# Image attention: scores in two banks of 333 columns, with the high queries on the keys' low halves as two products of 64 rows

## The chip, the cores and the metric

The program runs on one core of a Trainium2 chip. The metric is device time in microseconds (us) of one execution; given is the median of several. Matmuls run on TensorE (PE; its weight loads are listed apart as PEld), elementwise work on VectorE (DVE), ScalarE (ACT) and GpSimd (POOL); SyncE (SP) issues most DMA transfers. TensorE writes to PSUM, called `banks` here: eight banks of 512 fp32 columns on 128 partitions.

## The reference

The kernel computes four layers, each a gated attention followed by a gated feed-forward part, on an x of 4 batches by 512 tokens by 128. The change touches the first attention alone:

```python
def _L0_xattn_ref(image_embeds, latents, ln1_g, ln1_b, ln2_g, ln2_b, Wq, Wkv, Wo):
    DIM_HEAD, HEADS = 64, 16
    x = layer_norm(image_embeds, ln1_g, ln1_b)      # 4 x 154 x 128
    l = layer_norm(latents, ln2_g, ln2_b)           # 4 x 512 x 128
    q = l @ Wq
    kv = jnp.concatenate([x, l], axis=1) @ Wkv      # 666 keys
    k, v = jnp.split(kv, 2, axis=-1)
    # to heads: 4 x 16 x tokens x 64
    scale = 1.0 / np.sqrt(np.sqrt(DIM_HEAD))
    w = jnp.einsum('bhqd,bhkd->bhqk', q * scale, k * scale)
    w = jax.nn.softmax(w.astype(jnp.float32), axis=-1).astype(q.dtype)
    out = jnp.einsum('bhqk,bhkd->bhqd', w, v)
    return out.transpose(0, 2, 1, 3).reshape(B, S_lat, INNER) @ Wo

x = x + jnp.tanh(g_xattn[0]) * _L0_xattn_ref(ctx_1024, _layernorm(x, axis=-1), ...)
```

## The kernel before

The first attention ("image attention") is worked off in 32 groups (`GROUPS0`: 4 batches by 8 pairs of heads). A group has eight **subtiles** (256 in all, `SUBS`; number i): head 0 or 1 of the pair, and one of four tiles of 128 queries. Every subtile needs the scores of 128 queries against 666 keys (`KEYS0`: 512 of the tokens and 154 of the image), then a softmax and the product with the values.

fp32 accuracy is had from bf16 matmuls: queries and keys are split into a high half (the value rounded to bf16) and a low half (what is left). A head is 64 deep and the array has 128 rows, so one pass holds two products. For head h, `q[n % 2][:, h, :]` has the queries' high half in 64 of its rows and their low half in the other 64. `k[n % 2][:, h, part, :]` has the keys' high half (part 0) or low half (part 1) in both halves of the rows. A pass over part 0 and one over part 1 add up all four products of halves, in `image_scores_pe` (lines 741 to 750): four matmuls (L749), of 512, 512, 154 and 154 columns, all with the same 128 by 128 stationary operand. The columns 0 to 511 lie in one bank, 512 to 665 in the next; two such slots of two banks take turns.

The order of work is written out by hand; engines wait for one another through semaphores (`wait_ge`, `then_inc`). The loop of `image_pe` over steps i does on TensorE:

- the scores of subtile i (L749);
- in odd steps, for one head of an earlier unit of four subtiles, the product of the probabilities with the values (`image_weigh_pe`: L788, 30 small matmuls, sometimes L794 behind them);
- the turn of the probabilities of subtile i - 2 (`image_turn_pe`): four fp32 transposes into bank 4 (L760), one or more into bank 5 (L767, L769, L772);
- in even steps, one part of the projections for the next group (L520).

Bank 4 has one buffer. ACT copies it out (L947), and the next four transposes wait for that copy (`kept_a`).

DVE takes the negated maximum of the scores (L832), ACT the exponential with it as bias (L954); both read the 666 columns of a slot as one run. POOL splits the turned probabilities into halves (L1055) and gathers the last 32 of every row (L1061). For the next group ACT and DVE cut the projections into halves (L977, L914 for the queries; L983, L918 for the keys), and SP moves them between partitions: three transfers of 64 partitions for q (lines 1102 to 1105), four for k (L1109: two per head, 2664 bytes on each of 64 partitions). The first score of a group and head waits until the transfers of that head have landed (`in_place`).

In the part that follows and in later layers the kernel has matmuls with fewer than 128 rows or columns of the array in use. The profile shows them as rows*columns: 128*128 is the whole array, 128*64 and 128*32 fewer columns, 64*128 the upper 64 rows. L2993, L3024, L3025 and L2977 of the last layer are such lines and their neighbours.

## Time and profile before

| | |
|---|---|
| median of 3 runs | 1662.7 us (1659.42 to 1669.96) |
| the profiled execution | 1668.15 us |
| its span, first to last instruction | 1666.3 us |
| mean granted TensorE clock | 0.946 of full |
| score matmuls | from 34.9 to 636.9 us of the span |

The profile is of one execution; all rows below are of it. Times in its views are us from the start of its span, unless marked ns. The matmuls are pipelined: the next one starts while the last columns of the one before are still on their way through the array, so the distance from start to start tells what a matmul costs in a stream, and its own duration is longer than that. A row of several merged instructions shows the time from the first start to the last end.

### The profile page before, as it was taken

What the parts mean: (1) busy time and instruction counts of PE and PEld (TensorE: products, weight loads), DVE (VectorE), ACT (ScalarE), POOL (GpSimd) and SP (SyncE); (2) the same over time, 40 slices, a digit from 0 to 9 for tenths busy, and PEclk for the clock granted to TensorE, in tenths of its full rate; (3) what the DMA queues carried; (4) which work ended last, traced back from release to release, by engine and by line L of the source; (5) the groups of instructions that cost most, each with busy time, mean ns of one, the idle gap of its engine ahead of it and who ended that gap; (6) DMA issues with size and microseconds to landing.
All of it is one profiled execution on the core that took longest, in us unless ns stands there. A gap on an engine that the chain in (4) does not pass through costs nothing.

```text
span 1666.3 us, 37005 instructions
## 1 busy us (share of the span) xinstructions
PE 1448.2 (87%) x13825; PEld 979.5 (59%) x13825; DVE 1115.8 (67%) x2918; ACT 780.2 (47%) x1565; POOL 878.1 (53%) x1308
## 2 busy tenths in 40 slices
PE   3999999999999998887888789989986777789997
PEld 2777777777777776655566545544453343435555
DVE  4889788878777675544664577755454657587763
ACT  2777767767775562543223445554234444311211
POOL 3789888978776694364225663414014322253330
PEclk9999999999999999998999999999997789988998
DMA  7233222211121121241000000000000000000000
GB/s 276 69 118 93 87 86 53 52 45 47 46 61 44 44 63 44 61 150 42 1 1 1 9 9 2 2 1 1 1 1 1 1 1 1 1 0 1 7 7 14
DMA packets 35479, 64.31 MB, mean 39 GB/s; under 512 B 7535, under 2 KB 25042, under 8 KB 34147
## 3 DMA queue, kind: packets, MB, share of 16 engines
q1 hardware_dynamic: 33831, 59.83, 12.2%
q8 instruction: 113, 1.85, 0.5%
q0 software_dynamic: 1472, 2.12, 0.4%
q14 instruction: 63, 0.52, 0.1%
HBM read 30.64 MB, written 12.66 MB: 26 GB/s over the span
## 4 chain that ended last, share of the span: by engine, by line
PE 33%; DVE 12%; ACT 3%; POOL 3%; issue 2%; DMA 0%; DVEq 0%; ACTq 0%; POOLq 0%
PE banks L520 9%; PE banks L2202 3%; PE banks L2188 2%; PE banks L3050 2%; PE banks L2709 1%; PE banks L2993 1%; PE banks L2155 1%; PE banks L2715 1%; DVE work L2285 1%; PE banks L495 1%; PE banks L1755 1%; PE banks L2191 1%; PE banks L2977 1%; DVE work L3213 1%; DVE xn L466 1%
## 5 line engine op out<-in xcount | busy, mean ns | idle before, releaser
L1055 POOL TENSOR_TENSOR work<-work 128x512 bf16<-128x512 f32 (+1 forms) x512 | 358.7, 723 | 78.2 <-ACT work L947 77.3
L832 DVE TENSOR_REDUCE work<-banks 128x1 f32<-128x666 f32 x256 | 216.4, 845 | 65.1 <-PE banks L749 62.5
L954 ACT ACTIVATE work<-banks,work 128x666 f32<-128x666 f32 x256 | 208.1, 813 | 31.8 <-DVE work L832 24.9
L947 ACT ACTIVATE work<-banks 128x512 f32<-128x512 f32 x256 | 152.8, 597 | 146.5 <-PE banks L760 146.1
L460 POOL TENSOR_TENSOR norm_room<-norm_room,minus_half 128x4 f32<-128x4 f32 (+1 forms) x56 | 53.1, 950 | 289.6 <-DVE norm_room L435 168.8
L749 PE MATMUL banks<-work 128*128 128x512 bf16 (+1 forms) x1024 | 188.8, 307 | 3.8 <-DMA work<-work 3.7
L760 PE MATMUL banks<-const,work 128*128 128x128 f32 x1024 | 159.6, 279 | 15.4 <-ACT work L947 12.2
L520 PE MATMUL banks<-work,weights_b 128*128 128x512 bf16 (+1 forms) x840 | 152.8, 340 | 9.9 <-ACT work L1340 4.3
L749 PEld LDWEIGHTS banks<-work 128*128 128x128 bf16 x1024 | 96.2, 98 | 83.1 <-DMA work<-work 4.7
L2285 DVE TENSOR_REDUCE work<-banks 128x2 f32<-128x308 f32 x192 | 86.4, 471 | 83.0 <-PE banks L2155 58.3
L788 PE MATMUL banks<-work 128*128 128x65 bf16 (+1 forms) x3840 | 136.5, 193 | 3.1 <-POOL work L1055 1.8
L760 PEld LDWEIGHTS banks<-const,work 128*128 128x128 f32 x1024 | 111.6, 142 | 35.3 <-issue 34.3
L788 PEld LDWEIGHTS banks<-work 128*128 128x128 bf16 x3840 | 129.1, 97 | 3.8 <-POOL work L1055 3.4
L520 PEld LDWEIGHTS banks<-work,weights_b 128*128 128x128 bf16 (+1 forms) x840 | 81.5, 98 | 76.4 <-issue 12.5
L3262 POOL TENSOR_TENSOR work<-work 128x512 bf16<-128x512 f32 x64 | 67.5, 1060 | 98.7 <-DVE work L3213 98.6
L2260 ACT ACTIVATE work<-banks 128x256 f32<-128x256 f32 (+1 forms) x256 | 88.5, 380 | 62.3 <-PE banks L2191 34.9
L840 DVE COPY work<-banks 128x128 f32<-128x128 f32 x256 | 73.3, 286 | 28.4 <-PE banks L769 14.9
L2188 PE MATMUL banks<-work 128*128 128x256 bf16 (+1 forms) x256 | 69.7, 292 | 9.2 <-ACT work L2252 5.3
L495 PE MATMUL banks<-const,xn 128*128 128x128 f32 x176 | 32.2, 307 | 48.7 <-DVE xn L466 19.9
L769 PE MATMUL banks<-const,work 128*128 128x128 f32 x256 | 70.2, 274 | 0.5 <-DVE scratch L1203 0.5
L2155 PE MATMUL banks<-work 128*128 128x308 bf16 x192 | 60.0, 317 | 7.6 <-DVE work L2285 7.5
L501 ACT ACTIVATE xt<-banks 128x512 f32<-128x512 f32 x28 | 16.7, 597 | 104.8 <-PE banks L495 104.8
(460 smaller groups left out, 3289.6 us busy)
## 6 DMA issues: line engine op xcount, KB each, us to landing
work<-work SPq DMA_DIRECT2D x128, 166.5 KB, 2.7
sorted<-in_pads SPq DMA_DIRECT2D x10, 838.5 KB
weights_b<-in_weights SPq DMA_DIRECT2D x1, 4120.0 KB, 23.8
work<-scratch SPq DMA_DIRECT2D x64, 64.0 KB, 1.9
weights_b<-in_weights SPq DMA_DIRECT2D x1, 2824.0 KB, 12.3
weights_a<-in_weights SPq DMA_DIRECT2D x1, 2056.0 KB
weights_a<-in_weights SPq DMA_DIRECT2D x1, 2050.0 KB, 9.9
work<-work SPq DMA_DIRECT2D x32, 64.0 KB, 1.9
```

The costliest lines, as they stand in the source:

```text
L520: m = pe.matmul(out, left(a), right(b), start=start and n == 0, stop=stop and n == 2)
L749: m = pe.matmul(slot[:, a:z], lhs, k[:, h, part, a:z], start=part == 0, stop=part == 1)
L760: m = pe.transpose(ps[:, t * P:(t + 1) * P], prob[:, t * P:(t + 1) * P], self.eye)
L788: pe.matmul(self.out_heads[:, 2 * j + h, 0:width], parts[:, h, t, j * P:(j + 1) * P, of_probs], v[:, t, of_values, h, 0:width], start=(h, ...
L832: ve.tensor_reduce(self.neg_max[i % 4], self.slot[i % 2][:, 0:KEYS0], AX_X, ALU.max, negate=True).then_inc(self.mark("max"))
L947: ac.activation(self.probs_t[u % 2][:, h, 0:4, j * P:(j + 1) * P], self.bank_a.rearrange("p (t n) -> p t n", t=4), ACT.Copy).then_inc(self ...
L954: ac.activation(self.probs[i % 3], self.slot[i % 2][:, 0:KEYS0], ACT.Exp, bias=self.neg_max[i % 4]).then_inc(self.mark("exp"))
L1055: po.tensor_tensor(parts[:, :, :, 0], exact, parts[:, :, :, 1], ALU.subtract).then_inc(self.mark(event, i - 3))
L2155: m = pe.matmul(bank, a.q4[b % 2][:, group, c * P:(c + 1) * P], a.keys[b % 3][:, 2 * g:2 * g + 2, :].rearrange("p h k -> p (h k)"), start= ...
L2188: m = pe.matmul(bank, left, a.q4[b % 2][:, g, cols], start=True, stop=s != 4)
L2260: ac.activation(out, self.bank_of(k, HALF)[0:rows_n, :], ACT.Exp).then_inc(self.mark("exp4", s, n))
L2285: ve.tensor_reduce(a.most[u % 2][:, c % 2, 2 * g:2 * g + 2], self.bank_of(a.score_banks[n % 3], 2 * CTX).rearrange("p (h k) -> p h k", h=2 ...
```

## The change

The keys' low halves are no longer held in both halves of the rows. `k[n % 2][:, h, :]` now has 666 columns with the high halves of all keys in both halves of the rows, and 334 columns behind them: in the upper 64 rows the low halves of the keys 0 to 333, in the lower 64 rows those of the keys 332 to 665. The scores of a subtile lie in two banks: keys 0 to 332 at the columns 1 to 333 of the first, keys 333 to 665 at the columns 1 to 333 of the second. They are made by four matmuls of 334 columns. Two use all 128 rows of the array (both halves of the queries on the keys' high halves, one for each bank). Two use 64 rows: the queries' high half on the low halves of the keys, the first in the upper 64 rows for the first bank, the second in the lower 64 rows for the second bank. The product of low half with low half is left out. The built program gives the last two the array positions (0, 0) and (64, 0), each 64 by 128. For a high half on each side of the partitions, the queries' high half is kept whole in a buffer of its own, `q_both`; the queries' low half is written straight into `q`, so that `q_part` and its two waits go. DVE's maximum and ACT's exponential read the two banks as 2 by 333. SP's transfers for k become six: per head one of 1000 columns, one of 666 and one of 334.

```diff
@@ -15,6 +15,7 @@
 I32 = mybir.dt.int32
 U16 = mybir.dt.uint16
 AX_X = mybir.AxisListType.X
+AX_XY = mybir.AxisListType.XY
 
 P = 128
 BATCH, SEQ, CTX = 4, 512, 154
@@ -37,6 +38,7 @@
 PAIRS = H0 // 2
 KEYS0 = SEQ + CTX
 KT0 = -(-KEYS0 // P)
+PART0 = KEYS0 // 2
 EXPERTS, FF = 8, 512
 ROOM = 10
 SORT, SORTED = 256, 15
@@ -564,11 +566,11 @@
     def image_memory(self):
         self.work_at = self.stage0_at
         self.q = [self.place(2, SEQ, dt=BF16) for _ in range(2)]
-        self.k = [self.place(2, 2, KEYS0, dt=BF16) for _ in range(2)]
+        self.q_both = [self.place(SEQ, dt=BF16) for _ in range(2)]
+        self.k = [self.place(2, KEYS0 + PART0 + 1, dt=BF16) for _ in range(2)]
         self.v = [self.place(KT0 + 1, 2, 2 * VALUE, dt=BF16).rearrange("p t s (h d) -> p t s h d", h=2) for _ in range(3)]
         self.probs = [self.place(KEYS0) for _ in range(3)]
         self.k_parts = self.place(2, KEYS0, dt=BF16)
-        self.q_part = self.scratch[:, 2:4, :].rearrange("p t n -> p (t n)").bitcast(BF16)
         self.probs_t = [self.place(2, KT0 - 1, 2 * P) for _ in range(2)]
         self.rest, self.rest_t = ([self.place(P) for _ in range(2)] for _ in range(2))
         self.ctx_last = self.place(2, P + 32, dt=BF16)
@@ -735,7 +737,11 @@
 
     def in_place(self, n, h):
 
-        return self.at(f"dma_head{n % 2}{h}", 48 * (n // 2 + 1))
+        return self.at(f"dma_head{n % 2}{h}", 64 * (n // 2 + 1))
+
+    def scores_of(self, i):
+
+        return self.slot[i % 2].rearrange("p (k n) -> p k n", k=2)[:, :, 1:PART0 + 1]
 
     def image_scores_pe(self, pe, i):
         u, n, b, p, h, j = self.image_sub(i)
@@ -743,10 +749,14 @@
         if i % 8 in (0, 2):
             pe.wait_ge(*self.in_place(n, h))
         slot = self.bank(pe, 2 * (i % 2), "exp", i + 1, n=2)
-        lhs, k = self.q[n % 2][:, h, qt * P:(qt + 1) * P], self.k[n % 2]
-        for a, z in ((0, SEQ), (SEQ, KEYS0)):
-            for part in (0, 1):
-                m = pe.matmul(slot[:, a:z], lhs, k[:, h, part, a:z], start=part == 0, stop=part == 1)
+        rows, k = slice(qt * P, (qt + 1) * P), self.k[n % 2][:, h, :]
+        first, second = slot[:, 1:PART0 + 2], slot[:, BANK:BANK + PART0 + 1]
+        whole, both = self.q[n % 2][:, h, rows], self.q_both[n % 2][:, rows]
+        top, bottom = slice(0, D0), slice(D0, 2 * D0)
+        pe.matmul(first, whole, k[:, 0:PART0 + 1], start=True, stop=False)
+        pe.matmul(second, whole, k[:, KEYS0 - PART0 - 1:KEYS0], start=True, stop=False)
+        pe.matmul(first, (both, whole)[h][top, :], k[top, KEYS0:], start=False, stop=True)
+        m = pe.matmul(second, (whole, both)[h][bottom, :], k[bottom, KEYS0:], start=False, stop=True)
         m.then_inc(self.mark("scores"))
 
     def image_turn_pe(self, pe, i):
@@ -829,7 +839,7 @@
                                  ALU.mult).then_inc(self.mark("divided"))
             if i < SUBS:
                 ve.wait_ge(*self.at("scores", i + 1))
-                ve.tensor_reduce(self.neg_max[i % 4], self.slot[i % 2][:, 0:KEYS0], AX_X, ALU.max, negate=True).then_inc(self.mark("max"))
+                ve.tensor_reduce(self.neg_max[i % 4], self.scores_of(i), AX_XY, ALU.max, negate=True).then_inc(self.mark("max"))
             if i >= 1 and (i - 1) // 8 + 1 < GROUPS0 and (i - 1) % 8 in (0, 2, 4, 6):
                 self.image_lows_ve(ve, (i - 1) // 8 + 1, (i - 1) % 8 // 2)
             if 2 <= i < SUBS + 2:
@@ -908,10 +918,7 @@
             return
         if part == 0:
             ve.wait_ge(*self.at("q_high", n + 1))
-            if n >= 1:
-                for h in (0, 1):
-                    ve.wait_ge(*self.in_place(n - 1, h))
-            ve.scalar_tensor_tensor(self.q_part, side, D0 ** -0.5, self.q[n % 2][:, 0, :], ALU.mult, ALU.subtract).then_inc(self.mark("q_low"))
+            ve.scalar_tensor_tensor(self.q[n % 2][:, 1, :], side, D0 ** -0.5, self.q_both[n % 2], ALU.mult, ALU.subtract).then_inc(self.mark("q_low"))
         else:
             k, c0, width = self.k_parts, (0, SEQ)[part - 1], (SEQ, CTX)[part - 1]
             ve.wait_ge(*(self.at("k_high", 2 * n + 1) if part == 1 else self.at("v_kept", 4 * n + 3)))
@@ -951,7 +958,7 @@
                     ac.wait_ge(*self.at("turned_b", i - 1))
                     ac.wait_ge(*self.at("gathered", i - 3))
                 ac.wait_ge(*self.at("max", i + 1))
-                ac.activation(self.probs[i % 3], self.slot[i % 2][:, 0:KEYS0], ACT.Exp, bias=self.neg_max[i % 4]).then_inc(self.mark("exp"))
+                ac.activation(self.probs[i % 3].rearrange("p (k n) -> p k n", k=2), self.scores_of(i), ACT.Exp, bias=self.neg_max[i % 4]).then_inc(self.mark("exp"))
             if i == 4:
                 ac.wait_ge(*self.at("dma_rows", 16))
                 ac.activation(self.gates[:, :], self.rows[:, 0:8], ACT.Tanh).then_inc(self.mark("gates"))
@@ -974,7 +981,7 @@
         if part == 0:
             if n >= 2:
                 ac.wait_ge(*self.at("scores", 8 * n - 8))
-            ac.activation(self.q[n % 2][:, 0, :], side, ACT.Copy, scale=D0 ** -0.5).then_inc(self.mark("q_high"))
+            ac.activation(self.q_both[n % 2], side, ACT.Copy, scale=D0 ** -0.5).then_inc(self.mark("q_high"))
         elif part in (1, 2):
             c0, width = (0, SEQ)[part - 1], (SEQ, CTX)[part - 1]
             if part == 1 and n >= 1:
@@ -1097,16 +1104,17 @@
         self.loads(sp)
         top, bottom = slice(0, D0), slice(D0, 2 * D0)
         for n in range(GROUPS0):
-            q, k, low = self.q[n % 2], self.k[n % 2], self.q_part
+            q, both, k, parts = self.q[n % 2], self.q_both[n % 2], self.k[n % 2], self.k_parts.rearrange("p s n -> p (s n)")
             sp.wait_ge(*self.at("q_low", n + 1))
-            sp.dma_start(q[top, 1, :], q[bottom, 0, :]).then_inc(self.mark("dma_swap", n=16), 16)
-            sp.dma_start(q[bottom, 1, :], low[bottom, :]).then_inc(self.mark(f"dma_head{n % 2}1", n=16), 16)
+            sp.dma_start(q[top, 0, :], q[top, 1, :]).then_inc(self.mark("dma_swap", n=16), 16)
+            sp.dma_start(q[bottom, 0, :], both[top, :]).then_inc(self.mark(f"dma_head{n % 2}0", n=16), 16)
             sp.wait_ge(*self.at("dma_swap", 16 * (n + 1)))
-            sp.dma_start(q[bottom, 0, :], low[top, :]).then_inc(self.mark(f"dma_head{n % 2}0", n=16), 16)
+            sp.dma_start(q[top, 1, :], both[bottom, :]).then_inc(self.mark(f"dma_head{n % 2}1", n=16), 16)
             sp.wait_ge(*self.at("k_low", 2 * n + 2))
             for h, own in ((0, top), (1, bottom)):
-                for half in (top, bottom):
-                    sp.dma_start(k[half, h, :, :], self.k_parts[own, :, :]).then_inc(self.mark(f"dma_head{n % 2}{h}", n=16), 16)
+                sp.dma_start(k[top, h, :], parts[own, 0:KEYS0 + PART0 + 1]).then_inc(self.mark(f"dma_head{n % 2}{h}", n=16), 16)
+                sp.dma_start(k[bottom, h, 0:KEYS0], parts[own, 0:KEYS0]).then_inc(self.mark(f"dma_head{n % 2}{h}", n=16), 16)
+                sp.dma_start(k[bottom, h, KEYS0:], parts[own, 2 * KEYS0 - PART0 - 1:]).then_inc(self.mark(f"dma_head{n % 2}{h}", n=16), 16)
             if 2 <= n < 2 + PAD_PARTS:
                 self.pads_sp(sp, n - 2)
 
```

On PE, two subtiles in a row in the middle of a group, the second with the product with the values behind it. Before (L749 scores, L760 and L769 turn, L520 projection for the next group, L788 product with the values):

```order
L769 MATMUL banks<-const,work 128x128
L749 MATMUL banks<-work 128x512 x2
L749 MATMUL banks<-work 128x154 x2
L760 MATMUL banks<-const,work 128x128 x4
L769 MATMUL banks<-const,work 128x128
L520 MATMUL banks<-weights_c,weights_a 128x512 x2
L520 MATMUL banks<-weights_c 128x512
L749 MATMUL banks<-work 128x512 x2
L749 MATMUL banks<-work 128x154 x2
L788 MATMUL banks<-work 128x65 x2
```

After (L756 to L759 scores, L770 turn to bank 4, L777 and L779 turn to bank 5, L522 projection, L798 product with the values):

```order
L756 MATMUL banks<-work 128x334
L757 MATMUL banks<-work 128x334
L758 MATMUL banks<-work 128x334
L759 MATMUL banks<-work 128x334
L770 MATMUL banks<-const,work 128x128 x4
L777 MATMUL banks<-const,work 128x128 x2
L779 MATMUL banks<-const,work 128x128
L522 MATMUL banks<-weights_c,weights_a 128x512 x2
L522 MATMUL banks<-weights_c 128x512
L756 MATMUL banks<-work 128x334
L757 MATMUL banks<-work 128x334
L758 MATMUL banks<-work 128x334
```

The score matmuls keep their place in the order; their number per subtile stays four, and the operations on both sides of them are the same (in the second piece it is a step with one turn more). The last two of each four are those of 64 rows.

On SP, the transfers of one group. Before:

```order
L1102 DMA work<-work 64x512
L1103 DMA work<-scratch 64x512
L1105 DMA work<-scratch 64x512
L1109 DMA work<-work 64x1332 x4
L1102 DMA work<-work 64x512
```

After:

```order
L1109 DMA work<-work 64x512
L1110 DMA work<-work 64x512
L1112 DMA work<-work 64x512
L1115 DMA work<-work 64x1000
L1116 DMA work<-work 64x666
L1117 DMA work<-work 64x334
L1115 DMA work<-work 64x1000
L1116 DMA work<-work 64x666
L1117 DMA work<-work 64x334
```

Four transfers for k have become six; the first three of the six are head 0's.

## Rows read from the trace of the kernel before

**Rows 1.** The page: busy time of each engine, share of the span, instructions.

```profile
PE 1448.2 (87%) x13825; PEld 979.5 (59%) x13825; DVE 1115.8 (67%) x2918; ACT 780.2 (47%) x1565; POOL 878.1 (53%) x1308
```

**Rows 2.** Busy time by stretch: the image attention, then what follows it.

```profile
core 0: us, PE busy (x) PEld busy (x) DVE busy (x) ACT busy (x) POOL busy (x), PEclk, DMA share, GB/s
35.00:637.00 602.00, 572.80 (x7660) 455.89 (x7661) 478.31 (x1176) 412.64 (x735) 491.66 (x899) 0.99 0.24 63
```

**Rows 3.** Who waited for whom, 35 to 637 us: total, times, longest.

```profile
ACT work L947 <- PE banks L760: 143.7, 241, 3.1
PEld banks L760 <- issue: 33.5, 113, 0.9
...
PE banks L760 <- ACT work L947: 11.6, 60, 0.7
PE banks L749 <- DMA work<-work: 3.7, 3, 2.6
```

**Rows 4.** PE's timeline over a group's end: start, us, line, operation, [idle before <-releaser].

```profile
306.70 0.73 PE L749 MATMUL banks<-work 128*128 128x512 bf16 x4
307.59 0.63 PE L760 MATMUL banks<-const,work 128*128 128x128 f32 x4 [0.16 <-ACT work L947]
...
308.85 0.73 PE L749 MATMUL banks<-work 128*128 128x512 bf16 x4
309.41 1.06 PE L788 MATMUL banks<-work 128*128 128x65 bf16 x30
...
310.99 0.38 PE L749 MATMUL banks<-work 128*128 128x512 bf16 x1
```

**Rows 5.** The same timeline, asked to end behind one, two, three score matmuls.

```profile
308.85 0.38 PE L749 MATMUL banks<-work 128*128 128x512 bf16 x1
308.85 0.59 PE L749 MATMUL banks<-work 128*128 128x512 bf16 x2
308.85 0.66 PE L749 MATMUL banks<-work 128*128 128x512 bf16 x3
```

**Rows 6.** PE's timeline in the last layer: 64-row matmuls between whole-array ones.

```profile
1495.10 0.27 PE L3024 MATMUL banks<-work 64*128 64x128 f32 x1
...
1495.37 0.38 PE L2977 MATMUL banks<-work,const_b 96*128 96x512 bf16 x1
1495.68 0.37 PE L3024 MATMUL banks<-work 64*128 64x128 f32 x1
...
1495.90 0.49 PE L3024 MATMUL banks<-work 64*128 64x128 f32 x3
1496.32 0.23 PE L3025 MATMUL banks<-const_b 128*128 128x128 bf16 x1
```

**Rows 7.** PE's timeline in the last layer: 64-column matmuls between whole-array ones.

```profile
1563.29 1.52 PE L520 MATMUL banks<-work,weights_a 128*128 128x512 bf16 x6
1564.74 0.88 PE L2993 MATMUL banks<-work,weights_a 128*64 128x512 bf16 x6
1565.56 0.82 PE L2977 MATMUL banks<-work,const_b 96*128 96x512 bf16 x3
```

**Rows 8.** The page's groups: count, busy, mean ns, idle before.

```profile
L832 DVE TENSOR_REDUCE work<-banks 128x1 f32<-128x666 f32 x256 | 216.4, 845 | 65.1 <-PE banks L749 62.5
L954 ACT ACTIVATE work<-banks,work 128x666 f32<-128x666 f32 x256 | 208.1, 813 | 31.8 <-DVE work L832 24.9
L947 ACT ACTIVATE work<-banks 128x512 f32<-128x512 f32 x256 | 152.8, 597 | 146.5 <-PE banks L760 146.1
L749 PEld LDWEIGHTS banks<-work 128*128 128x128 bf16 x1024 | 96.2, 98 | 83.1 <-DMA work<-work 4.7
L501 ACT ACTIVATE xt<-banks 128x512 f32<-128x512 f32 x28 | 16.7, 597 | 104.8 <-PE banks L495 104.8
```

**Rows 9.** Weight loads by form, whole span.

```profile
L3024 PEld LDWEIGHTS banks<-work 64*128 64x128 f32 x56 | 9.6, 205 | 5.1 <-issue 2.6 <-DVE work L3228 0.8
```

**Rows 10.** SP's timeline at the end of a group, and the page's DMA issues with KB and us to landing.

```profile
306.40 2.38 SPq L1109 DMA_DIRECT2D work<-work  x4
...
work<-work SPq DMA_DIRECT2D x128, 166.5 KB, 2.7
work<-scratch SPq DMA_DIRECT2D x64, 64.0 KB, 1.9
```

## The prediction

> **What bounds the kernel now.** I read the page's busy shares first: PE leads with 87% of the span [rows 1]. That is an average over many layers, so next the busy time of the stretch that the change touches: from 35 to 637 us PE is busy 573 of 602 us, POOL 492, DVE 478, ACT 413, and the granted clock is 0.99 of full [rows 2]. PE bounds the stage, and 256 subtiles in 602 us make 2.35 us each. Then the waits of the stage, to see where PE isn't the bound: 113 times its weight load for the turn (L760) stood still, 33.5 us in all or 0.30 us each; PE itself sat idle before L760 for 11.6 us, with ACT's copy L947 as releaser [rows 3]. The timeline shows the place [rows 4]. At 306.70 a subtile's scores start, and the transposes behind them start only at 307.59, 0.89 us later. At 308.85 the scores are followed by the product with the values, at 309.41, 0.56 us later, without a gap. So there are two kinds of steps. In even steps the turn stands right behind the scores and waits for ACT to clear bank 4, which holds the turn of the step before; that copy takes 0.60 us [rows 8] after the transposes it reads, and the 0.56 us of scores run inside this time, with about 0.33 us to spare. In odd steps the values follow at once and every ns of scores counts. There are 128 even steps, 113 of which show the wait; 128 + 15 = **143 subtiles** have scores on the path.
>
> **The scores in a stream.** Start to start, four matmuls take 0.56 us. One of 512 columns takes 0.59 - 0.38 = 0.21, one of 154 takes 0.66 - 0.59 = 0.07 [rows 5]. By a line through these, 334 columns take 0.07 + (180 / 358) x 0.14 = 0.14 us. The change makes three such lengths of the four matmuls if the two 64-row ones run side by side: 3 x 0.14 = 0.42 us, 0.14 less than before.
>
> Do they run side by side? The trace of before has no pair in the upper and lower rows. The nearest row is the pairs in the left and right columns: six L2993 matmuls of 512 columns with 64 columns of the array take 0.88 us together, where six whole-array ones take 1.52 us [rows 7]. Three lengths, not six: pairs run at once. Both products here write to different banks and their positions in the array don't overlap, so I take 0.14 for the pair. The bound on the other side is 0.28, one after the other.
>
> **The price of changing the array's form.** This is what the column count hides. In the last layer, a 512-column L2977 (whole array) starts at 1495.37 and the 64-row L3024 behind it at 1495.68: 0.31 us, where L2977 follows L2977 after (0.82 - 0.38) / 2 = 0.22 us [rows 6, 7]. So going to 64 rows costs 0.09. Coming back: L3024 follows L3024 after (0.49 - 0.27) / 2 = 0.11 us (0.27 is the length of its later, shorter records), so the last of the three starts at 1496.12, and the whole-array L3025 at 1496.32, 0.20 later [rows 6]: again 0.09. Going to 64 columns shows the same: the last of six L520 starts at 1563.29 + 1.52 - 0.38 = 1564.43, and L2993 at 1564.74, 0.31 later against some 0.22 [rows 7]; coming back, 1565.56 against 1564.74 + 0.88 - 0.39 = 1565.23, that is 0.33 [rows 7]. Four places, four times 0.09 to 0.11 over the normal distance. I take 0.095 for each change. Nothing queued behind hides it, since in these rows weight loads and matmuls stood ready as well.
>
> Each subtile now has two changes of form, into 64 rows behind the second matmul and out of them before whatever follows: 2 x 0.095 = 0.19 us against the 0.14 saved. In the stream a subtile's scores take 0.42 + 0.19 = 0.61 us instead of 0.56: **0.05 us more**. Of these 143 are on the path: 143 x 0.05 = +7.2 us. In the other 113 the scores grow by 0.05 inside a wait of about 0.33 and cost nothing; ACT's copy is released by PE's turn of the step before, which the change doesn't touch, so the wait just gets shorter. The last matmul of a subtile ends a little earlier than before, measured from the first (0.14 + 0.14 + 0.095 and its own length, against 0.49 and its own), so DVE and ACT get their scores no later.
>
> The Trainium skill bears on this in TensorEngine Tiling (Array Packing), section Key Properties: a change of tiling mode, as against a change of tile, drains TensorE. Rows 6 and 7 agree, at 0.09 to 0.11 us each time. The same page's section Theoretical Speedup gives up to twice the throughput where a dimension is 64 or less, and counts no change of form.
>
> **Weight loads.** There are four per subtile as before. Those of the whole array have a mean of 98 ns [rows 8] and hide behind the matmul ahead of them. For 64 rows the only row is fp32, 205 ns [rows 9], and its matmuls still follow each other after 0.11 us, so two loads don't stand in line for their whole length. The second load of the pair can hold up the second product by anything from nothing to one load of 98 ns; I take nothing, as the column pairs show (three pairs in 0.88 us leave 0.88 - 0.39 = 0.49 for two steps, 0.245 each, against 0.22: some 0.03 per pair). With 0.03 the sum is 143 x 0.08 = +11 us, with 0.098 it is 143 x 0.15 = +21 us.
>
> **DVE and ACT** read 2 by 333 instead of 666 columns: as many elements. ACT's copy that writes four pieces of 128 takes 597 ns, as its plain copy of 512 does [rows 8], so pieces as such cost nothing there; for DVE no row tells, but it has 124 us of slack in 602 [rows 2]. Without that cover 0.05 us more on each of 256 would be 13 us; it is hidden by PE. DVE's wait for the last group's transfers before the queries' low half goes, and with it nothing that anyone waited for; PE did the waiting.
>
> **SP's queue and the transfers.** SP spends some 0.6 us on each issue (four in 2.38 us, the last one's record included), and a transfer lands 2.7 us after its issue, one of 64 KB after 1.9 [rows 10]. Head 0's last transfer for k was the second, 306.40 + 0.64 + 2.7 = 309.7, and the first score of that group starts at 310.99 [rows 4, 10]: 1.25 us to spare. Now it is the third, issued 0.64 later but of 43 KB only: landing near 306.40 + 1.28 + 1.9 = 309.6, or 310.4 if small ones took 2.7 as well. Both are in time. Behind it on SP stand the transfers of head 1, needed two steps (4.7 us) later, and a block of pads; nobody waits for those. PE waited for a transfer three times in the stage, 3.7 us in all [rows 3]; where it did, the extra issue can add 0.64 us each, 0 to +2 us. I take 0.
>
> **The sum.** +7.2 us on the profiled execution's 1668.15 us is 1675; its span is 1666.3, with 1.9 around it. That execution lies 5.5 above the median of the runs, which I go by: 1662.7 + 7.2 = **1670 us**. The later layers have nothing of the change in them. About 1% (16.6 us) is what a measurement of this kernel tells from no change; its own runs spread over 10 us.
>
> **Rivals.** (1) The changes of form cost nothing here, because the next loads and matmuls are already queued and the two forms of 64 rows lie inside the same array. Then the stream is 0.42 us, 0.14 less in the 143 subtiles: -20 us, **1643**. It can't be more, since the 113 others wait for ACT whatever the scores cost. If one of the two changes is free, 143 x (0.14 - 0.095) = -6 us, 1656. Against both speak all four places in rows 6 and 7. The Trainium skill, TensorE: Matmul & The Clock Gate, Part 3, gives a pack's span as one matmul and about 4 ns for each further tile, with no term for getting in and out; with it this rival would come out. Rows 7 bear out the pair and contradict the missing term. Chance 0.12, both versions.
>
> (2) Slower: the two 64-row products don't overlap, fully or in part, because the second one's weights are only loaded once the first streams, or because rows are not like columns. The place is between the third and the fourth score matmul. Fully serial, the stream is 0.56 + 0.19 = 0.75 us, +0.19 in 143 subtiles: +27 us, **1690**; held up by one load of 98 ns, +21 us, 1684. In the 113 waiting subtiles 0.19 still fits into 0.33. It decides against the kernel by over 1% from a delay of 0.07 us on (143 x 0.12 = 17 us). For it speaks that no row shows a pair by rows, against it the column pairs. Chance 0.16.
>
> (3) The transfers land late: if every k transfer took 2.7 us from its own issue and SP's issues got longer, head 0's third one would eat the 1.25 us to spare in the tighter groups. Half a us in 31 groups would be +16 us, 1679. The 43 KB size and the 25% fewer bytes (8000 instead of 10656 per partition and group) speak against it. Chance 0.05.
>
> **How the numbers follow.** The forecast, 1670 with 1662 to 1676 for its own terms (0 to +2 for transfers, 0 to +4 for the pair's second load), has 0.67. Rival 1 has 0.12, of which about half (both changes free) is faster by over 1%; with an unseen cause, such as a kinder layout in PSUM, faster has 0.09. Rival 2 lies above +1% in nearly all its cases, 0.15, and rival 3 in some, 0.02: slower has 0.17. The rest, 0.74, is within 1%. The range from 1650 to 1688 takes in one free change, and the held-up pair; what it leaves out is both free (0.07) and fully serial with late transfers (0.07).
>
> **What would show it.** In the new profile, L758 should start some 0.235 us behind L757 (0.14 + 0.095), L759 within 0.03 us of L758, and what follows some 0.235 us behind that where it doesn't wait. The scores' first start to L798's should be 0.61 us. The wait before the turn in even steps should shrink from 0.30 by about 0.05. PE's stage should end near 644 us instead of 637, DVE's and ACT's means at 845 and 813 ns should stand. I am wrong if L759 starts 0.1 us or more behind L758, if L757 to L758 is 0.14, or if PE waits for DMA at the start of every group.

## The result

The changed kernel is slower by a little: 1679.08 us median of 7 runs (1673.57 to 1687.22), the kernel before 1666.37 us of 7 (1659.42 to 1672.84). The ratio is 1.0064, 95% interval 1.0035 to 1.0092, so +5.8 to +15.3 us, around +10.7; the two medians lie 12.7 apart. Differences below go by the ratio, unless it says "by the medians". Forecast were +7.2 us and 1670 us in all, with 1662 to 1676 for the prediction's own terms and 1650 to 1688 as the range. The time lies in the range and 3 us above the narrower band; 3.7 us of the distance to 1670 are the kernel before itself, whose median was 1662.7 in the three runs that the forecast stood on.

The page of the changed kernel, shares first ([rows 1] are those of before), then the groups that answer to [rows 8]:

```profile
PE 1444.2 (86%) x13721; PEld 953.0 (57%) x13825; DVE 1114.6 (67%) x2918; ACT 780.1 (47%) x1565; POOL 877.7 (53%) x1308
...
L842 DVE TENSOR_REDUCE work<-banks 128x1 f32<-128x666 f32 x256 | 216.4, 845 | 64.4 <-PE banks L759 62.7
L954 ACT ACTIVATE work<-banks 128x512 f32<-128x512 f32 x256 | 152.8, 597 | 155.3 <-PE banks L770 154.9
L961 ACT ACTIVATE work<-banks,work 128x666 f32<-128x666 f32 x256 | 208.1, 813 | 29.1 <-DVE work L842 22.2
```

PE's busy time reads 4 us less than before for a longer kernel. 104 of its 13825 matmul records are missing in this trace, so the 4 us are no measurement, and this view can't tell the change. DVE's maximum and ACT's exponential have the same means, 845 and 813 ns; reading 2 by 333 costs neither anything.

What happened stands in the changed kernel's timeline, an even step's scores and turn, then an odd step's scores and values (start, us, line, operation):

```profile
318.52 0.31 PE L756 MATMUL banks<-work 128*128 128x334 bf16 x1
318.66 0.31 PE L757 MATMUL banks<-work 128*128 128x334 bf16 x1
318.90 0.31 PE L758 MATMUL banks<-work 64*128 64x334 bf16 x1
318.90 0.31 PE L759 MATMUL banks<-work 64*128 64x334 bf16 x1
319.41 0.63 PE L770 MATMUL banks<-const,work 128*128 128x128 f32 x4 [0.20 <-ACT work L954]
...
320.63 0.31 PE L756 MATMUL banks<-work 128*128 128x334 bf16 x1
320.78 0.31 PE L757 MATMUL banks<-work 128*128 128x334 bf16 x1
321.02 0.31 PE L758 MATMUL banks<-work 64*128 64x334 bf16 x1
321.02 0.31 PE L759 MATMUL banks<-work 64*128 64x334 bf16 x1
321.26 0.32 PE L798 MATMUL banks<-work 128*128 128x65 bf16 x5
```

Read it by starts. L757 comes 0.14 us behind L756: 334 columns. L758 comes 0.24 behind L757: 0.14 for the columns and 0.10 for going to 64 rows. L759 starts together with L758, so the upper and lower rows do work side by side. The values start 0.24 behind that: 0.14 and 0.10 for going back. The sum is 321.26 - 320.63 = 0.63 us where before it was 0.56 [rows 4]; the medians over the odd steps are 0.629 and 0.566. In the even step the turn starts 0.89 us behind the first score, exactly as before [rows 4], with PE idle for ACT's copy: the whole price has gone into that wait.

The waits of the stage, 35 to 642 us (total, times, longest), answer to [rows 3]:

```profile
ACT work L954 <- PE banks L770: 152.5, 241, 1.6
...
PEld banks L758 <- issue: 71.6, 256, 0.5
...
PEld banks L770 <- issue: 42.1, 129, 0.9
...
PE banks L770 <- ACT work L954: 13.0, 59, 0.7
PE banks L756 <- DMA work<-work: 3.5, 2, 3.2
```

The new row is the weight load of L758, which stood still 256 times for 71.6 us, 0.28 each. Most of that is time in which the matmuls before it still stream, so it isn't the price, but it is the signature of the change of form. The weight loads of the odd step above:

```profile
320.64 0.10 PEld L757 LDWEIGHTS banks<-work 128*128 128x128 bf16 x1
321.01 0.09 PEld L758 LDWEIGHTS banks<-work 64*128 64x128 bf16 x1 [0.28 <-issue]
321.01 0.09 PEld L759 LDWEIGHTS banks<-work 64*128 64x128 bf16 x1
321.26 0.11 PEld L798 LDWEIGHTS banks<-work 128*128 128x128 bf16 x2 [0.15 <-issue]
```

L757's load starts 0.14 us ahead of its matmul. Those of L758 and L759 are recorded 4 to 5 ns ahead of theirs, all 256 times, and so is the first one behind the pair here. A load isn't taken ahead over a change of form. The turn's load stands still 129 times instead of 113, now in every even step, and for 0.33 us each instead of 0.30: it too is no longer taken ahead. So this row can't be read as the room that is left before the turn. For a transfer PE waited no more often.

Laid side by side, subtile by subtile, the time from one subtile's first score to the next one's grew by a median of 0.075 us in the odd steps and by 0.000 us in the even ones (medians over 127 and 128 distances, worked out from the starts of L749 and L756). 128 x 0.075 = 9.6 us, inside the interval of the result. Of the 0.075, the scores have 0.063 (0.629 - 0.566 in the starts); the remaining 0.014 falls on the first values matmuls (0.039 and 0.036 us apart, before 0.029 each), whose weight loads used to be taken ahead during the scores.

A median hides a minority. Ten even steps (8, 76, 78, 92, 140, 142, 156, 204, 206 and 220) grew by 0.11 to 0.15 us, and all ten are among the few in which the turn's load showed no wait before. About a dozen others shrank by as much; why stays open.

The profiled pair alone shows less, and why is worth a look. The last subtile's scores started at:

```profile
L756 PE MATMUL banks<-work x256: 303/306/487, 35.5 to 641.4; 128*128 128x334 bf16 x128
```

That is 641.4 us, and in the kernel before 636.3 (its last of four at 636.9), 5 us. In 514 to 574 us the profiled run of before had a dip of the granted clock which the changed kernel's didn't have (before, then changed; the column behind POOL is the clock):

```profile
514.00:574.00 60.00, 56.01 (x708) 45.06 (x705) 44.03 (x118) 35.25 (x64) 37.14 (x72) 0.94 0.18 46
```

```profile
514.00:574.00 60.00, 55.65 (x749) 42.81 (x751) 44.04 (x118) 36.13 (x65) 37.47 (x71) 1.00 0.14 34
```

The record of the granted clock has 6.8 us at half clock (1.2 GHz) in the stage of before and none in the changed kernel's; steps 222 to 224 lie there and at its edge, and together they are 2.2 us longer in the kernel before. Step 87 was 0.7 us longer there as well; the rest of the distance from 5 to 9.6 us stays unexplained. A comparison of two single profiles would have halved the effect.

### The profile page after: what moved, and what is told of

It is laid out like the page before. It is cut to its first block, busy times and chain, and to the rows that moved or that the text cites. A ratio compares the mean times of both kernels' runs of the same rounds, so it can differ in the third digit from the quotient of the medians.

```text
span 1671.8 us, 36934 instructions
## 1 busy us (share of the span) xinstructions
PE 1444.2 (86%) x13721; PEld 953.0 (57%) x13825; DVE 1114.6 (67%) x2918; ACT 780.1 (47%) x1565; POOL 877.7 (53%) x1308
## 4 chain that ended last, share of the span: by engine, by line
PE 34%; DVE 10%; ACT 4%; POOL 2%; issue 2%; DVEq 0%; ACTq 0%; POOLq 0%
PE banks L522 8%; PE banks L2210 4%; PE banks L2196 2%; PE banks L3058 2%; PE banks L2717 1%; PE banks L2163 1%; PE banks L3001 1%; PE banks L2723 1%; PE banks L497 1%; DVE work L3221 1%; PE banks L2199 1%; PE banks L1763 1%; PE banks L307 1%; PE banks L1687 1%; PE banks L2985 1%
## 5 line engine op out<-in xcount | busy, mean ns | idle before, releaser
L770 PE MATMUL banks<-const,work 128*128 128x128 f32 x1024 | 159.6, 278 | 18.4 <-ACT work L954 13.6
L522 PE MATMUL banks<-work,weights_b 128*128 128x512 bf16 (+1 forms) x830 | 150.0, 337 | 13.6 <-ACT work L1348 6.9
L798 PE MATMUL banks<-work 128*128 128x65 bf16 (+1 forms) x3840 | 138.1, 193 | 2.9 <-POOL work L1062 1.9
L798 PEld LDWEIGHTS banks<-work 128*128 128x128 bf16 x3840 | 123.2, 97 | 22.4 <-issue 17.5
L770 PEld LDWEIGHTS banks<-const,work 128*128 128x128 f32 x1024 | 110.6, 141 | 43.9 <-issue 42.9
L522 PEld LDWEIGHTS banks<-work,weights_b 128*128 128x128 bf16 (+1 forms) x840 | 81.0, 98 | 78.1 <-issue 13.7
L756 PE MATMUL banks<-work 128*128 128x334 bf16 x256 | 78.8, 308 | 3.6 <-DMA work<-work 3.5
L758 PE MATMUL banks<-work 64*128 64x334 bf16 x256 | 80.4, 314 | 0.0
L759 PE MATMUL banks<-work 64*128 64x334 bf16 x256 | 80.3, 313 | 0.0
L757 PE MATMUL banks<-work 128*128 128x334 bf16 x256 | 78.9, 308 | 0.0
L779 PE MATMUL banks<-const,work 128*128 128x128 f32 x256 | 69.9, 273 | 0.4 <-DVE scratch L1211 0.4
```

The source lines that it names most:

```text
L522: m = pe.matmul(out, left(a), right(b), start=start and n == 0, stop=stop and n == 2)
L758: pe.matmul(first, (both, whole)[h][top, :], k[top, KEYS0:], start=False, stop=True)
L759: m = pe.matmul(second, (whole, both)[h][bottom, :], k[bottom, KEYS0:], start=False, stop=True)
L770: m = pe.transpose(ps[:, t * P:(t + 1) * P], prob[:, t * P:(t + 1) * P], self.eye)
L798: pe.matmul(self.out_heads[:, 2 * j + h, 0:width], parts[:, h, t, j * P:(j + 1) * P, of_probs], v[:, t, of_values, h, 0:width], start=(h, ...
```

## The experiments

All eleven ran in 5 rounds beside the kernel before. The base of the first six is the changed kernel with the keys' low halves held in full in both halves of the rows, as the kernel before has them, so that the form of the last two score matmuls is free to choose. For the room, `q_both[0]` lies in the old `q_part` and `ctx_last` behind `ctxn_parts`; nothing else is moved. `low_first` and `low_second` are the first and the last 334 columns of these low halves.

**e1, the pair with full k.**

```diff
-        self.k = [self.place(2, KEYS0 + PART0 + 1, dt=BF16) for _ in range(2)]
+        self.k = [self.place(2, 2 * KEYS0, dt=BF16) for _ in range(2)]
...
+                for half in (top, bottom):
+                    sp.dma_start(k[half, h, :], parts[own, :]).then_inc(...)
```

> The changed kernel with the keys' low halves held in full in both halves of the rows again and four k transfers per group instead of six; the score matmuls are the changed kernel's. Theory (the two changes of the array's form per subtile are the whole cost, 0.075 us in each odd step): same as the changed kernel, +9 to +11 us over the kernel before. Rival (the six transfers of the k halves or the shorter k cost it): within 3 us of the kernel before.

Measured: 1671.76 us against 1665.31, ratio 1.0044 (1.0018 to 1.0071), +7.3 us. That is less than the +9 to +11 expected and more than the rival's 3. Odd steps are longer by a median of 0.075 us, even ones by -0.001. The slowdown stays when the six transfers are four again, so most of it is not theirs. Whether the 3 us between this and the changed kernel's +10.7 are the transfers' isn't settled: the intervals overlap, and the steps are the same in both traces.

**e2, whole array throughout.**

```diff
-        pe.matmul(first, (both, whole)[h][top, :], k[top, low_first], start=False, stop=True)
-        m = pe.matmul(second, (whole, both)[h][bottom, :], k[bottom, low_second], start=False, stop=True)
+        pe.matmul(first, whole, k[:, low_first], start=False, stop=True)
+        m = pe.matmul(second, whole, k[:, low_second], start=False, stop=True)
```

> As e1, but the low products use all 128 rows again: four whole-array matmuls of 334 columns per subtile, in two banks of 333, no change of form (the low-by-low product is back in). Theory: 1336 columns against 1332, so -1 to +3 us against the kernel before, and the score matmuls 0.14 us apart throughout. Rival (two banks of 333 and their reading in two pieces cost): +8 us or more, as the changed kernel.

Measured: ratio 1.0008 (0.9982 to 1.0035), no difference that shows, as expected. Its timeline:

```profile
319.87 0.31 PE L757 MATMUL banks<-work 128*128 128x334 bf16 x1
320.01 0.31 PE L758 MATMUL banks<-work 128*128 128x334 bf16 x1
320.16 0.31 PE L764 MATMUL banks<-work 128*128 128x334 bf16 x1
320.30 0.30 PE L765 MATMUL banks<-work 128*128 128x334 bf16 x1
```

0.14, 0.15, 0.14 apart. The two banks of 333 cost nothing that shows; odd steps are 0.008 us longer than before.

**e3 and e4, the pair in odd or in even steps only.** Shown against e2; e4 has `i % 2 == 0` in place of e3's condition:

```diff
+        if i % 2 == 1:
+            pe.matmul(first, (both, whole)[h][top, :], k[top, low_first], start=False, stop=True)
+            m = pe.matmul(second, (whole, both)[h][bottom, :], k[bottom, low_second], start=False, stop=True)
+        else:
             pe.matmul(first, whole, k[:, low_first], start=False, stop=True)
             m = pe.matmul(second, whole, k[:, low_second], start=False, stop=True)
```

> As e2, but in odd steps (values right behind the scores) the low products are the pair of 64 rows. Theory: all of the cost stands in odd steps, so +8 to +11 us, as e1. Rival (each of 256 subtiles pays the same): about half of e1's, +4 to +6 us.

> As e2, but only in even steps (the turn waits for ACT behind the scores) are the low products the pair of 64 rows. Theory: the changes of form lie inside the wait for bank 4, so -1 to +3 us, as e2. Rival (each subtile pays the same): +4 to +6 us.

Measured: e3 1.0038 (1.0013 to 1.0062), +6.3 us; e4 1.0004 (0.9983 to 1.0025), +0.7 us. e3 missed its +8 to +11 and lies by its time alone as near to the rival's +4 to +6; the intervals of the two runs overlap as well. The steps tell them apart. In e3 the odd steps grew by 0.075 us and the even ones by 0.000 (medians, against the kernel before); in e4 by 0.008 and 0.000, although its even steps hold the same pair and the same two changes of form as e1's. Step by step against e2, 115 of e4's 128 even steps are within 0.02 us, and 11 are longer by 0.10 to 0.11 each, 1.2 us together: the ten named above and 232. The ten had no wait before the turn, neither in the kernel before nor in e2. So the pair costs by where it stands, and this is what the split into 143 on the path and 113 off it claimed.

**e5, both products in the upper 64 rows.**

```diff
+        upper = (both, whole)[h][top, :]
+        pe.matmul(first, upper, k[top, KEYS0:KEYS0 + PART0 + 1], start=False, stop=True)
+        m = pe.matmul(second, upper, k[top, 2 * KEYS0 - PART0 - 1:2 * KEYS0], start=False, stop=True)
```

> As e1, but both products of 64 rows use the upper 64 rows of the array, so that they can't run side by side. It tells what the overlap is worth. Theory: the fourth score matmul starts 0.14 us behind the third, odd steps grow by 0.14, +16 to +20 us over e1, even steps still fit into the wait. Rival (the pair's overlap gave nothing on the path): as e1.

Measured: ratio 1.0196 (1.015 to 1.0243), +32.7 us, or +28.8 by the medians. That is 25 us more than e1 by the ratios and 22 by the medians, above the +16 to +20 expected; the intervals of the two leave room for both. The overlap is worth 0.14 us on every odd step, 128 x 0.14 = 18 us:

```profile
321.06 0.31 PE L758 MATMUL banks<-work 128*128 128x334 bf16 x1
321.30 0.31 PE L760 MATMUL banks<-work 64*128 64x334 bf16 x1
321.45 0.30 PE L761 MATMUL banks<-work 64*128 64x334 bf16 x1
321.69 0.98 PE L800 MATMUL banks<-work 128*128 128x65 bf16 x27
```

L761 now starts 0.15 behind L760 instead of with it, and the price of the two changes of form is unchanged (0.24 on each side). Odd steps grew by 0.215 us, even ones by 0.001 in the median: also 0.2 us more fit into the wait. This is the mechanism of rival 2, and 128 x 0.215 = 27.5 us is the size that rival 2 had (+27).

**e6, three whole-array matmuls.**

```diff
-        pe.matmul(first, (both, whole)[h][top, :], k[top, low_first], start=False, stop=True)
-        m = pe.matmul(second, (whole, both)[h][bottom, :], k[bottom, low_second], start=False, stop=True)
+        m = pe.matmul(first, whole, k[:, KEYS0:KEYS0 + PART0 + 1], start=False, stop=True)
```

> Three whole-array matmuls of 334 columns per subtile and no fourth: the keys' low halves of the second 333 keys are left out of the scores, so part of the computation is missing. It has the changed kernel's column time (0.42 us) without any change of form, and shows what the change would be worth if changes of form were free. Theory: 0.14 us less than before in the odd steps, nothing in the even ones, -16 to -20 us against the kernel before. Rival (every subtile is on PE's path): -32 to -36 us.

This kernel leaves out the keys' low halves of the second 333 keys. Measured: ratio 0.9912 (0.9882 to 0.9941), -14.7 us, or -15.7 by the medians, just short of the -16 to -20 expected. Odd steps are 0.135 us shorter, even ones 0.000. It has the time that the changed kernel's columns would need if changes of form were free: about -15, not the -35 that 0.135 for all 256 subtiles would be. The waits, 35 to 621 us, show where the other half went:

```profile
PEld banks L770 <- issue: 66.6, 114, 1.3
...
PE banks L770 <- ACT work L954: 30.1, 113, 1.0
```

PE's own idle time before the turn went from 11.6 us in 60 times [rows 3] to 30.1 in 113, and its load's from 33.5 to 66.6 us: what was saved in an even step turned into waiting for bank 4.

**e7 and e8, the wait filled.** In e7 (the kernel before) and e8 (the changed one) the projection of even steps stands ahead of the turn:

```diff
+            project = i // 8 + 1 < GROUPS0 and i % 8 in (0, 2, 4, 6)
+            if project and not self.image_late(i):
+                self.image_project_pe(pe, i // 8 + 1, i % 8 // 2)
             if 2 <= i < SUBS + 2 or self.rest_due(i) is not None or self.mix_due(i) is not None:
                 self.image_turn_pe(pe, i)
...
-            if i // 8 + 1 < GROUPS0 and i % 8 in (0, 2, 4, 6):
+            if project and self.image_late(i):
                 self.image_project_pe(pe, i // 8 + 1, i % 8 // 2)
```

> The kernel before, with one edit: in even steps the part of the projection for the next group stands between the scores and the turn instead of behind the turn (except in the few steps that share its bank with the output). The 0.30 us wait for bank 4, 113 times, should be filled. Theory: -25 to -34 us against the kernel before. Rival (another engine or wait takes its place): less than 10 us gained.

> The changed kernel with the edit of e7. With the wait filled, the scores are on the path in even steps too, so the change should cost about twice what it did. Theory: e8 is 15 to 19 us slower than e7 (256 times 0.062 to 0.075). Rival (the cost is not one of each subtile on the path): e8 is 7 to 11 us slower than e7, as the changed kernel was against before.

Both expectations missed; e7 came out as its rival, e8 below its theory and its rival. e7: ratio 0.9968 (0.9945 to 0.9992), -5 us by the ratio and -9.5 by the medians, not -25 to -34. e8: 0.9983 (0.9955 to 1.0011). e8's median is 4.7 us above e7's, not 15 to 19 and not 7 to 11: against e7 its odd steps are longer by a median of 0.074 us, its even ones shorter by 0.017. Even steps still had a wait to hide in. The weight loads' waits of e7, 35 to 637 us:

```profile
PEld banks L520 <- DVE work L924: 10.6, 28, 1.4
PEld banks L520 <- issue: 10.4, 25, 0.8
PEld banks L495 <- issue: 7.6, 6, 1.5
PEld banks L791 <- POOL work L1058: 4.5, 4, 1.3
PEld banks L520 <- DVE work L921: 4.4, 9, 0.7
PEld banks L763 <- issue: 3.7, 11, 0.8
```

The wait before the turn (L763) is gone, 3.7 us from 33.5, and one before the projection (L520) has come, 25 us in its three rows. Bank 7 is freed by ACT's copy of the part before and DVE's low half behind it, and ACT makes that copy at the end of its step, behind the copy of the turn and the exponential. A new wait took the place of the old one; e9 puts this to the test. e7's stage ended 12 us earlier than that of before (last score at 624.5, before 636.9), of which the runs kept 5 to 9; the rest lies behind the stage, where nothing was edited, and stays unexplained.

**e9 and e10, ACT's keep moved as well.** In `image_ac`, `image_keep_ac` of the same steps goes ahead of the copy of the turn, for the kernel before (e9) and the changed one (e10):

```diff
+            project = i // 8 + 1 < GROUPS0 and i % 8 in (0, 2, 4, 6)
+            if project and not self.image_late(i):
+                self.image_keep_ac(ac, i // 8 + 1, i % 8 // 2)
             if 2 <= i < SUBS + 2:
...
-            if i // 8 + 1 < GROUPS0 and i % 8 in (0, 2, 4, 6):
+            if project and self.image_late(i):
                 self.image_keep_ac(ac, i // 8 + 1, i % 8 // 2)
```

> e7, and ACT keeps the projection (its copies out of bank 7) ahead of the copy of the turn and the exponential, not behind them. In e7 the projection waited for bank 7, whose release ran over ACT's late copies and DVE's L921 and L924. Theory (that wait took the place of the one for bank 4): the wait shrinks, -15 to -30 us against the kernel before. Rival (the later turn itself costs as much elsewhere): as e7, -5 to -9 us.

> The changed kernel with both edits of e9. Theory: with all 256 subtiles nearer to the path, 12 to 19 us slower than e9, against the 9 to 11 between the changed kernel and the one before. Rival (only odd steps pay, whatever stands behind the scores of even ones): 9 to 10 us slower than e9.

Measured: e9 1638.83 us, ratio 0.9852 (0.981 to 0.9894), -25.3 us by the medians: faster than both kernels, with the score matmuls of before. e10 1654.42, ratio 0.9945 (0.992 to 0.997): 15.6 us above e9 by the medians. Both are as expected. The waits of weight loads in e9, 35 to 612 us, and then in e10, 35 to 628 us:

```profile
PEld banks L495 <- issue: 8.9, 6, 1.6
PEld banks L520 <- issue: 6.4, 14, 1.0
...
PEld banks L763 <- issue: 3.4, 10, 0.7
```

```profile
PEld banks L761 <- issue: 72.3, 256, 0.5
...
PEld banks L522 <- issue: 21.4, 115, 0.8
```

In e9 neither the turn nor the projection waits for long. With little wait to hide in, the 64-row pair costs 15.6 us instead of 7 to 11: the even steps pay too. The steps show it. Against e9, e10's odd steps are longer by a median of 0.074 us and its even ones by 0.074 as well (from each subtile's second weight load, since e9's trace lacks many score matmuls' records), 7.7 and 8.0 us in all. (L761 is e10's first matmul of 64 rows; L522 is the projection, which stands right behind the pair in even steps and whose load is no longer taken ahead.)

**e11, e6 with both edits.** No new lines: e6's score matmuls and e9's order.

> e6 (three whole-array matmuls, the low halves of the second 333 keys left out of the scores, so part of the computation is missing) with both edits of e9. It shows whether a saving of 0.14 us per subtile reaches the end once the wait is filled. Theory: 18 to 36 us faster than e9. Rival (POOL or DVE, busy over 80% of the stage, become the bound): under 10 us faster than e9.

It leaves out what e6 leaves out. Measured: 1614.8 us, ratio 0.9712 (0.9675 to 0.9748), 24.0 us faster than e9 by the medians, where e6 was 15.7 faster than before. Busy time in its stage (PE, PEld, DVE, ACT, POOL):

```profile
35.00:592.00 557.00, 522.51 (x7376) 443.52 (x7437) 475.67 (x1179) 408.70 (x737) 491.98 (x902) 0.99 0.25 68
```

24 of the 34.6 us (256 x 0.135) that the shorter scores offer arrive at the end. POOL is now busy 492 of 557 us and DVE 476, 88% and 85%; that they take the missing 10 us is argued from these shares, not shown.

## Why the prediction was right, point by point

**The two kinds of steps** held, and are shown: e3 against e4, and e6's half gain. The count was off by a little. I took 143 subtiles on the path, 128 odd and 15 even ones that showed no wait. The even steps' growth of 0.000 us in the median can't tell 15 steps of 128, but the steps one by one can: 11 of them grew in e4 over e2, by 0.11 us each, and ten of these had shown no wait. That makes 139, and each of the 11 pays 0.11 where an odd step pays 0.075.

**The scores in a stream.** 0.14 us for 334 columns: measured 0.141. Pairs side by side: L759 starts within 4 ns of L758 (e5 shows what it is worth). Taken from pairs of columns, the row held for pairs of rows.

**The price of changing form.** 0.095 each way from four places of the last layer; measured 0.098 on the way in and 0.103 on the way out. 0.61 us forecast for the scores, 0.629 measured. Where the sum had +0.05 per subtile it was +0.063. What the 0.1 us consist of is open: the load that isn't taken ahead takes 93 ns by its record, close to the price, but no run tells the load from an emptying of the array. The Trainium skill's sentence on draining (TensorEngine Tiling (Array Packing), section Key Properties) agrees with the trace as far as that: the first 64-row matmul starts 0.098 us behind the columns before it, the median of 256.

**The mis-sized term** is what follows the scores. The +0.05 us per subtile left out that the values matmuls behind them begin with loads that nobody took ahead: 0.014 us per odd step. With 0.075 for 0.05 in 128 odd steps and 0.11 in 11 even ones the sum is 9.6 + 1.2 = 10.8 instead of 7.2, and the runs have +10.7. Some of that agreement is luck: a few steps shrank, and the interval is 9 us wide.

**One sign pointed the wrong way.** The wait before the turn was to shrink from 0.30 us by about 0.05, and its row grew to 0.33. The idea of the room stood (e5 put 0.14 us more into it and the even steps' median grew by 0.001), but the row measures the time between two weight loads, and behind the pair the turn's load is no longer taken ahead.

**DVE, ACT, transfers.** As forecast, nothing: 845 and 813 ns stand, e2 is level with before, PE waited for a transfer twice (three times before). The first scores start 0.55 us later (35.5 against 34.9). The one issue more doesn't explain it, since e1 and e2, with four transfers, start at 35.5 and 35.4 as well; the cause stays open.

**Rival 1** (form changes cost nothing) fell by the timeline, and e6 gave its size: about -15 us where it had -20. **Rival 2** (pair in series) fell by L759's start; its price, +27, is near e5's +28.8 to +32.7. **Rival 3** (late transfers) fell with the two waits in the table above and with e1.

**What I didn't foresee** was outside the prediction: that filling the wait for bank 4 would only uncover the one for bank 7 (e7), which took a second edit on another engine to clear (e9).

## What to carry to other kernels

Before a matmul is cut into pieces that share the array, count the changes of form as well as the columns: here two of them, 0.10 us each, against 0.14 saved by 330 columns less. By an estimate from these numbers, a visit to the smaller form pays from some 480 columns saved (0.20 / 0.14 x 334), which takes longer products or several pairs per visit; that wasn't tried. Look at what stands behind the matmuls before pricing a saving: the same 0.14 us was worth all of it in odd steps and nothing in nearly all even ones, and an edit of order alone (e9) gave 25 us where the edit of arithmetic lost 11.

## What the runs showed of the hardware

- Going from 128 by 128 to 64 by 128 of the array costs 0.098 us beyond the columns and going back 0.103, for bf16 matmuls of 334 columns (medians of 256 ways in and of 124 ways back, those of the odd steps). Weight loads aren't taken ahead across it: those of L758 start 4 to 5 ns before their matmuls, where L757's start 140 ns before.
- Two matmuls in the upper and lower 64 rows, into different banks, start 3 to 4 ns apart and have nearly the same length (mean 314 and 313 ns).
- Two matmuls in the same 64 rows follow each other after 0.152 us at 334 columns, where two of the whole array take 0.141 to 0.146.
